# Four-stage network on one core: side work of the experts' stage cut into five smaller portions per tile, late weights in smaller goes, down projection three tiles behind

## What is computed

```
x = x + tanh(g_xattn[0]) * linear_attention(ln(x), ctx)        # stage A
x = x + tanh(g_ffn[0])   * ffn(ln(x))                          # stage F, hidden 2048, gelu
x = x + tanh(g_xattn[1]) * softmax(ln(x) ctx^T, masked) ctx    # context attention
x = x + tanh(g_ffn[1])   * experts(ln(x))                      # stage E

experts(x): probs = softmax(x gate_weight^T)                   # 32 experts
            top 8 of them, normalised, summed by 8 groups -> w_tg
            h = x gate_up[g]^T; act = silu(gate) * up          # per group g, 192 wide
            out = sum_g w_tg * (act down[g]^T)
```

## Time and profile before

| | us |
|---|---|
| median of 3 runs | 1927.16 |
| lowest, highest | 1926.29, 1928.27 |
| the profiled execution | 1926.13 |
| its span | 1924.3 |
| TensorE busy in the span | 1804.9 (94%) |
| VectorE busy | 1154.5 (60%) |
| GpSimd busy | 652.0 (34%) |
| ScalarE busy | 599.5 (31%) |

### The profile page before, as it was taken

One profiled execution on the slowest core, in us unless ns is written; L12 is line 12 of the kernel. 1 busy time (PEld: TensorE's weight loads), 2 busy tenths in 40 slices (PEclk: granted clock), 3 DMA queues, 4 the chain that ended last, 5 costly groups with the idle time before them and its releaser, 6 DMA issues.

```text
span 1924.3 us, 29111 instructions
## 1 busy us (share of the span) xinstructions
PE 1804.9 (94%) x11224; PEld 1074.0 (56%) x11224; DVE 1154.5 (60%) x2332; ACT 599.5 (31%) x961; POOL 652.0 (34%) x603
## 2 busy tenths in 40 slices
PE   8699999999999999999988788989999999989898
PEld 3445555544444444444444465767677676767676
DVE  5667777654544545454345575857676766758554
ACT  2224434321111143411122343333333333333322
POOL 1123322321202075820203056363535344453533
PEclk9999999999999999999999899999999999999999
DMA  4124433342323314221120420211111111201111
GB/s 155 55 63 137 136 110 109 118 108 72 72 83 79 109 38 114 69 54 60 28 61 1 135 72 26 67 50 64 51 59 61 59 51 42 77 28 52 31 63 44
DMA packets 152620, 137.69 MB, mean 72 GB/s; under 512 B 79970, under 2 KB 96482, under 8 KB 152482
## 3 DMA queue, kind: packets, MB, share of 16 engines
q1 hardware_dynamic: 152482, 135.84, 23.6%
HBM read 103.17 MB, written 32.64 MB: 71 GB/s over the span
## 4 chain that ended last, share of the span: by engine, by line
PE 67%; DVE 11%; issue 10%; POOL 6%; ACT 2%; DMA 2%; SPq 1%; POOLq 0%; DVEq 0%; ACTq 0%
PE bank L1230 20%; PE bank L1333 14%; PE bank L1240 14%; PE bank L1431 8%; PE bank L1313 4%; PE bank L1249 3%; POOL arena L1193 2%; DVE arena L1654 1%; POOL arena L1199 1%; PE bank L1298 1%; PE bank L1279 1%; DVE arena L1721 1%; DMA arena<-x_after_ffn 1%; SPq L1002 1%; DVE arena L2046 1%
## 5 line engine op out<-in xcount | busy, mean ns | idle before, releaser
L1240 PE MATMUL bank<-arena 128*128 128x256 f16 x4032 | 516.6, 277 | 59.1 <-DVE arena L2029 43.6
L1230 PE MATMUL bank<-arena 128*128 128x512 f16 x2304 | 529.9, 382 | 6.0 <-DVE arena L1675 3.9
L1240 PEld LDWEIGHTS bank<-arena 128*128 128x128 f16 x4032 | 397.8, 100 | 180.1 <-DVE arena L2029 44.5
L1230 PEld LDWEIGHTS bank<-arena 128*128 128x128 f16 x2304 | 226.5, 98 | 273.5 <-issue 7.6
L1333 PE MATMUL bank<-arena 128*128 128x512 f16 x1536 | 353.8, 380 | 3.4 <-DVE arena L1882 2.0
L1431 PE MATMUL bank<-arena 128*128 128x512 f16 x1152 | 314.4, 383 | 11.2 <-POOL arena L1199 11.2
L1880 DVE TENSOR_SCALAR arena<-arena 128x512 f16<-128x512 f32 x128 | 79.7, 623 | 300.8 <-ACT arena L1535 295.2
L1333 PEld LDWEIGHTS bank<-arena 128*128 128x128 f16 x1536 | 150.3, 98 | 186.1 <-DVE arena L1882 5.3
L1193 POOL TENSOR_TENSOR arena<-arena 128x512 f32<-128x512 f32 x96 | 122.1, 1272 | 338.7 <-DVE arena L2046 338.7
L1535 ACT ACTIVATE arena<-bank,arena 128x512 f32<-128x512 f32 x128 | 99.2, 775 | 426.4 <-PE bank L1230 415.8
L1608 ACT ACTIVATE arena<-arena 128x512 f32<-128x512 f32 x96 | 69.2, 721 | 284.4 <-DVE arena L2040 284.4
(11 more groups left out here) (188 smaller groups left out, 1839.5 us busy)
## 6 DMA issues: line engine op xcount, KB each, us to landing
arena<-in_L_ffn_proj SPq DMA_DIRECT2D x64, 256.0 KB, 2.7
arena<-group_weights SPq DMA_DIRECT2D x64, 256.0 KB, 3.2
x_after_attention<-arena SPq DMA_DIRECT2D x8, 1024.0 KB, 5.1
arena<-x_after_attention SPq DMA_DIRECT2D x8, 1024.0 KB, 5.6
x_after_ffn<-arena SPq DMA_DIRECT2D x8, 1024.0 KB, 4.3
arena<-x_after_ffn SPq DMA_DIRECT2D x8, 1024.0 KB, 6.4
arena<-group_weights SPq DMA_DIRECT2D x64, 128.0 KB, 2.8
arena<-in_L_ffn_gate_up_proj SPq DMA_DIRECT2D x80, 96.0 KB, 2.0
```

Of the source, the lines that this page charges most:

```text
L1230: m = e.matmul(bank[b][:, :], wT[l][:, c, tile * P:(tile + 1) * P], y[h][:, c, :], start=n == 0, stop=n == NPASS - 1)
L1240: m = e.matmul(out, forms_of[j // 2][l][:, c, f, (j % 2) * P:(j % 2 + 1) * P], y[h][:, c0 + c, col:col + HT], start=n == 0, stop=n == 2 * ...
```

## The change

1. `apart` is called a fifth time per tile, right behind `p16` and ahead of the first part of the down projection. The slots of a tile are now A (behind `p16`), B (behind `down` part 0), C, D and E.
2. Big tasks of the side work are cut. The statistics come two and two. The softmax of the context attention becomes `scores` (to the subtraction), `sexp` (the exponential), `soft2` and `soft3`; the router's becomes `router`, `rexp`, `rout2`, `rout3` (the top 8) and `rout4`; the sums of quarters become `tsum` and `tsum2`. The operations and their semaphores are the same. Empty slots stand in other places; the list of a batch has its last task in slot D of its tenth tile, where it was slot B of the twelfth.
3. The down projection runs three tiles behind the products and not two, and the loop one round longer.
4. The late weights: four tiles of down weights are loaded ahead of stage F's end where eight were, the other four behind the loads of x; `finish_weights` gives each split, each low half and each piece a slot of its own. The pieces of the products' weights come in slots 38 to 47, the eighth to tenth tile, where they stood in the fifth to eighth.
5. In stage F's last batch five tasks per tile are taken where three were.

```diff
     def second_tasks(i):
         ph, b = i
-        slow = [None] if b > 0 else []
-        def stats():
-            for t in range(NT):
-                add("stat", i, t)
-            add("rs", i)
+        def stats(ts):
+            def go():
+                for t in ts:
+                    add("stat", i, t)
+                if NT - 1 in ts:
+                    add("rs", i)
+            return go
...
+        begin = [stats((0, 1)), stats((2, 3)), None]
         if ph == "L":
-            return [stats, *slow, norm(0), norm(1), turn(0, 2), *slow, turn(1, 3), *slow, turn(2), *slow, turn(3)]
+            return begin + [norm(0), norm(1), turn(0, 2), None, turn(1, 3), None, turn(2), None, turn(3), None]
         def sums(p):
-            return [lambda: add("tsum", b, p), lambda: add("thi", b, p), lambda: add("tlo", b, p)]
-        return [stats, *slow, norm(0), norm(2), turn(0, 1), *slow, turn(2, 3), *slow, *sums(0), *slow,
-                turn(1), *slow, turn(3), *slow, sums(1)[0], lambda: add("router", b, banks=1), *sums(1)[1:]]
+            return [lambda: add("tsum", b, p), lambda: add("tsum2", b, p), lambda: add("thi", b, p), lambda: add("tlo", b, p)]
...
+        return begin + [norm(0), norm(2), turn(0, 1), None, turn(2, 3), None, *s0, turn(1), None, turn(3), None,
+                        lambda: add("router", b, banks=1), both(step("rexp"), s1[0]), both(step("rout2"), s1[1]),
+                        both(step("rout3"), s1[2]), both(step("rout4"), s1[3])]
...
-        pause = [None] * (1 if b == 0 else 2)
...
-        return [L[0], both(split, L[1] or (lambda: None)), *L[2:], lambda: add("scores", b, banks=1), *pause,
-                lambda: add("pturn", b, banks=1), *pause[1:], *[read(t) for t in range(NT)], *M,
-                *pause, lambda: add("rturn", b, banks=1), *pause,
-                lambda: add("gsum", b, banks=1), groups]
+        return [*([None] * 5 if b == 1 else []), *L[:2], split, *L[3:], lambda: add("scores", b, banks=1), step("sexp"),
+                step("soft2"), step("soft3"), lambda: add("pturn", b, banks=1), None, *[read(t) for t in range(NT)], *M,
+                None, lambda: add("rturn", b, banks=1), None, lambda: add("gsum", b, banks=1), groups]
...
             if J == total - 1:
-                for t in range(8):
+                for t in range(4):
                     add("wload", W_OF["d", t])
             beside()
+            if side and J >= total - NH:
+                beside()
...
             beside()
-            if side and J >= total - NH:
-                beside()
+            for _ in range(2):
+                if side and J >= total - NH:
+                    beside()
     while side:
         f = side.pop(0)
         if f:
             f()
+    for t in range(4, 8):
+        add("wload", W_OF["d", t])
     add("xload", "E", 2)
...
+        for t in range(NR):
+            k = (0, 8, 24)[t // 4] + t % 4
+            put(k, "wsplit", W_OF["d", t])
+            put(k + 1, "wlo", W_OF["d", t])
+            if t >= 8:
+                put(16, "wload", W_OF["d", t])
+        s0 = W_OF["s", 4 * Q_EARLY]
+        for i in range(4):
+            put(29 if i < 2 else 33, "wload", s0 + i)
+        for i, k in ((0, 38), (2, 43)):
+            put(k, "fsplit", s0 + i)
+            put(k + 1, "flo", s0 + i)
+            put(k + 1, "fsplit", s0 + i + 1)
+            put(k + 2, "flo", s0 + i + 1)
+            put(k + 3, "fhi", s0 + i + 1)
+            put(k + 4, "flo2", s0 + i + 1)
...
-    for s in range(total + 2):
+    for s in range(total + 3):
...
         if s < total:
             add("p16", s, at=4)
-        down(s - 2, (0,))
+        apart()
+        down(s - 3, (0,))
         apart()
```

61 lines of the change are left out of this document (36 added, 25 removed).

## The result

| | before | after |
|---|---|---|
| median of the runs, us | 1926.7 | 1908.7 |
| lowest, highest, us | 1926.2, 1928.3 | 1906.2, 1911.0 |
| ratio, 95% interval | | 0.9906, 0.9891 to 0.9922 |
| span of the profiled execution, us | 1924.3 | 1907.7 |
| TensorE busy, us | 1804.9 | 1794.3 |

The change makes the kernel 18.1 us faster (four runs of each). The forecast of 1894 lay 15 us lower; 1908.7 is inside its range. Beside the lines named above, L1275 is the transposition of the rows (`turn` and `mturn`), L1383 `pturn`, L1389 `read` and L1696 `norm` in the changed kernel.

The account below looks back on a forecast made before the run. TensorE sets the time, with 8.8 us per block in six blocks not work. Gains of 22.5 (blocks), 7.2, 1.3, 2.3 and -0.4 sum to 32.9 us off 1926.1: 1893.2, median 1894, range 1874 to 1915.

Parts of the forecast that it names:

- the 4.33 and the 1.67 us: Waits per block at a first product behind the router and a seventh product behind the softmax; both were to go.
- the transposition of the probabilities: Softmax in each block: TensorE waits 2.2 us for the probabilities, where 1.67 was waited before.
- the new waits of a block: Per block: 2.2 us at the probabilities, 0.95 at the router's weights, 1.2 of smaller waits; sum 4.35.
- The clock: Falls to the lower clock level: 2.1 us per block before, 0.7 after, ends 0 and 2.1.
- Start: Experts' stage up to its fourth tile: earlier load of x and later statistics gain 7.2 us, ends 3 and 12.
- late weights: Rest of the first block, GpSimd full, 10.9 us idle there: gain 1.3 us, ends -6 and +10.
- end: Wait before the last tile's down projection, 2.33 us, goes with the projection a tile later: gain 2.3 us.
- Feed-forward stage: Last feed-forward block: some waits go, the probabilities come 2.5 us late; -0.4 us, ends -4 and +3.
- The second, crowding: Rival: tiles 4 to 9 overloaded, GpSimd's subtraction meets the router's multiply, one clock fall per block; 1913, chance 0.13.
- the third: Rival: a ScalarE table switch costs 1.28 us beyond its load in seven blocks, plus clock falls; 1913, chance 0.03.
- The fourth: Rival: several medium waits, clock falls behind probabilities, router weights and sums, 6.3 us per block; 1933, chance 0.05.
- the first: Rival: the spread works fully, probabilities and router weights come in time in all blocks; 1859, chance 0.13.

Follow-up runs that it names:

- Experiment 5: Changed kernel with GpSimd's low half of the mixed tile beside the end of the softmax held until the softmax is done: 1906.1 us.
- Experiment 10: Changed kernel with six empty slots per block, two GpSimd holds, third transposition of normalized rows one slot earlier, context 0 as before the change: 1876.9 us.
- experiment 7: Changed kernel with all eight late weights of the down projection issued ahead of the next x, as before the change: 1914.9 us.
- experiment 1: Changed kernel with the down projection two tiles behind the products again instead of three: 1917.6 us.
- experiment 2: Changed kernel with two empty slots ahead of the transposition of the probabilities in the experts' stage's seven softmaxes: 1908.4 us.
- experiment 4: Changed kernel with the softmax's small VectorE multiply by the scale folded into the 128x256 multiply behind it: 1908.5 us.
- exponential first (3): Changed kernel with ScalarE's exponential ahead of the silu of the same tile instead of behind it: 1916.4 us.
- first context (8): Changed kernel with the side work of context 0, in the feed-forward stage, in the steps and at the rate of before: 1907.7 us.
- three later (6): Changed kernel with two empty slots each ahead of the probabilities' transposition, the router and the router weights' transposition, contexts 2 to 7: 1898.8 us.
- held twice (9, 10): 9: changed kernel with six empty slots per block and GpSimd held at softmax and router chains, 1882.7 us; 10: also third `turn` earlier, old context 0, 1876.9 us.
- chain's end later (11, 12): 11: Experiment 10's kernel with the end of the router's chain two slots later, 1876.5 us; 12: also the late weights' pieces four slots earlier, 1882.1 us.

## Why the forecast was right in its sign and 15 us off in its size

**The long waits.** As forecast the 4.33 and the 1.67 us are gone, and the transposition of the probabilities and that of the router's weights are next late. The one at the router's was 1.02 us (0.95 forecast), the read 0.51 (0.5), the router 0.23 (0.4).

**The step that failed: the new waits of a block, 4.35 forecast, 6.42 measured.** In six blocks that is 12.4 us; 13.8 are missing there, and the two paragraphs on the uncounted time and on the clock account for the rest. Three terms were too small:

- the transposition of the probabilities, 2.98 instead of 2.2. The chain of the forecast is there step by step, but the rest of the softmax was taken from rows in which nothing ran on GpSimd. After the change it stands where GpSimd makes a low half, and costs 0.85 more. Experiment 5 took exactly that out.
- the fourth `turn`, 0.78 instead of 0.1. The copy of the third stands behind a silu in ScalarE's queue, and the silu waits for an add that stands, with two others, behind a norm which took 1.39 us beside GpSimd instead of 0.54 (first two rows below). Experiment 10 moved the copy ahead of the silu, and the wait fell to 0.20.
- the first `mturn`, 0.46, not forecast at all: a norm of 1.48 us beside GpSimd.

The forecast had seen this effect once, at the router's multiply, and had counted it as over by then; there it was right (0.29 us again, apart from one block). It had not asked for it at every chain that the change moves, though the trace before shows it there too: 23 of the 56 norms of the experts' stage start beside GpSimd and take 0.65 to 1.38 us, the others 0.54. In order of time in the kernel after: GpSimd and the norm ahead of the fourth `turn`, then the norm of 1.48 us and the next one, which GpSimd did not meet:

```profile
1311.76 1.15 POOL L1225 TENSOR_TENSOR arena<-arena 128x512 f16<-128x512 f32 x1 [1.59 <-ACT arena L1646]
1311.80 1.39 DVE L1696 TENSOR_SCALAR arena<-arena 128x512 f32<-128x512 f32 x1
...
1348.47 1.48 DVE L1696 TENSOR_SCALAR arena<-arena 128x512 f32<-128x512 f32 x1 [0.56 <-POOL arena L1125]
1350.21 0.53 DVE L1696 TENSOR_SCALAR arena<-arena 128x512 f32<-128x512 f32 x1
```

**Time that the brackets don't show.** A bracket counts from the end of the busy time of the matmul ahead, and that lies 0.16 us behind the point at which the next matmul would have started. Three rows ahead of the transposition of the probabilities:

```profile
1325.35 0.81 PE L1457 MATMUL bank<-arena 128*128 128x512 f16 x3
1326.00 1.47 PE L1266 MATMUL bank<-arena 128*128 128x256 f16 x12
1327.31 0.81 PE L1457 MATMUL bank<-arena 128*128 128x512 f16 x3
```

The first group of three is followed after 0.65 us, the second after 3.79: that is 3.14 us late, where the bracket says 2.98. So eight waits instead of four cost a block 0.65 us more, which the forecast did not count: it read the old waits from brackets and worked out the new ones from start to start. Added up from start to start, without the brackets and at the durations outside the falls of the clock, the 793 matmuls of a block take 95.27 us before and 96.02 after. Six times the difference is 4.5 us.

**The clock, forecast right before and too dear after.** With the falls in them, the same steps took 97.47 us a block before, on average. So the clock cost 2.20 us a block, where 2.1 had been counted; 95.27, 6.68 and 2.20 make the 104.15 of a block. After, 0.7 us a block was forecast, and one fall in six blocks cost 1.6 us, 0.26 a block: 3.2 us in the other direction. 12.4 + 4.5 - 3.2 = 13.7, and 13.8 are missing. That the last two nearly cancel is luck: the 0.7 was a choice between bounds, and by the table at the end the length of a wait would not have given a better one.

**Start, late weights, end.** 8.0 of 7.2 forecast, 3.0 of it by the queue (experiment 7). In the first block the router's wait, the tenth product's and `rturn`'s are 5.49, 3.72 and 1.35 us, 10.6 of 10.9 forecast, the first two behind GpSimd as it said and the third behind VectorE; with 1.3 forecast and nothing gained, this term is inside its bounds. At the end the wait is gone. The 0.48 us went too, but for another reason than the one given (experiment 1).

**Feed-forward stage.** -0.4 forecast, -2.3 in the profiled execution, -3.6 over all of them. The forecast let the transposition of its router's weights come free; it waits 3.46 us after the change, where none was. The stretch before and after, columns as in the earlier trace rows:

```profile
975.80:1076.80 101.00, 89.89 (x490) 42.78 (x488) 48.76 (x110) 26.62 (x36) 17.90 (x16) 0.93 0.16 45
```
```profile
976.00:1079.30 103.30, 87.95 (x490) 42.73 (x489) 47.33 (x110) 26.50 (x36) 18.32 (x16) 0.95 0.15 42
```

**The rivals.** The second, crowding, was nearest in its time (1913, as the third) and half right in its place: GpSimd beside VectorE's chains, but at the softmax and the norms, and without a fall of the clock in each block. The third fell with the size of the wait: 2.98 us, of which 0.85 is GpSimd's, leaves no room for 1.28 us more at the switch of tables. The fourth did not happen: no block of the six has more than one fall, in any kernel here. But experiment 2 shows that medium waits can do to the clock what one long wait did: there 2.09 us are followed by a fall in every block. In place of the first, the kernel of experiment 10 comes within 18 us of its 1859 by nothing but other places and two added waits of GpSimd: 1876.9 us, 2.7% under the kernel before and 1.7% under the changed one. What it still waits for is the first block (some 20 us of waits up to the twelfth tile, 5.5 and 3.1 of them behind GpSimd) and 1.81 us a block.

## What to carry to other kernels

Cutting side work and moving it forward pays only as far as each step's result is ready when its reader's place comes: sum each chain with the durations of its new neighbourhood, GpSimd's operations above all, count waits from start to start, and spend the free slots ahead of the readers. Where GpSimd's result has slack, let it wait for the chain. And forecast the clock as a cost of its own: a shorter wait may be the one that it falls behind.

## What the runs showed of the hardware

**VectorE beside GpSimd.** An operation of VectorE that starts while GpSimd subtracts or multiplies 128x256 or more ends 0.02 to 0.63 us behind the end of that one: 0.02 for 128x4, 0.15 for 128x128, 0.28 for a norm of 128x512, 0.55 for a mixing of 128x512. So it took 1.02 us for 128x4 (0.17 alone), 1.48 for the norm (0.54), 2.17 for a multiply of 128x128 (0.29). It happened to `tensor_scalar` with its input in SBUF and to operations with two SBUF inputs; it did not to VectorE's adds that read one operand from a bank (at most 0.42 us in the 60 first adds of a tile that started beside GpSimd), nor to reductions, the maximum of eight or the statistics of a norm. Nor did it to a `tensor_scalar` of a single column, seven times in the kernel before (GpSimd, VectorE):

```profile
1124.36 1.27 POOL L1193 TENSOR_TENSOR arena<-arena 128x512 f32<-128x512 f32 x1 [2.54 <-DVE arena L2046]
1124.93 0.21 DVE L1957 TENSOR_SCALAR arena<-arena 128x1 f32<-128x1 f32 x1
```

The Trainium skill (SBUF — State Buffer, Who interferes with whom) has a rule for it: the two engines share a pair of ports, which whoever starts first keeps for its whole instruction, against VectorE's two-port forms, `tensor_scalar` among them, and its operations with two SBUF inputs. The trace agrees, down to the four columns of the small multiply; for the single column it shows no meeting. The forecast had weighed the half of this rule on two inputs only; by the whole rule the norms and the small multiply would have been asked after too.

**The clock.** In the blocks a fall is 3.4 us long in the trace, in every other block of the kernel before 6.8. One of 3.4 costs a block 1.68 us (experiment 5: 103.29 less 101.61), in one block of experiment 4 only 1.3. How often one came beside the longest wait of a block, from within it to 1.4 us behind it, six blocks each:

| kernel | longest wait, us | blocks with a fall |
|---|---|---|
| before | 4.33 | 6 |
| exponential first (3) | 3.11 | 5 |
| after, and loads ahead (7), first context (8) | 2.98 to 3.00 | 1 each |
| two tiles behind (1) | 2.89 | 3 |
| folded (4) | 2.77 | 2 |
| held (5) | 2.14 | 3 |
| `pturn` later (2) | 2.09, and 1.67 ahead of it | 6 |
| three later (6) | 2.00, and 0.84 ahead of it | 3 |
| held twice (9, 10) | 1.81 | 0 |
| chain's end later (11, 12) | 1.43 | 0 |

Equal waits in one kernel come with a fall in some blocks and not in others, in a regular turn (experiments 5 and 6), so the length of a wait doesn't decide it alone. What else does was not settled.
